# Cross-attention: one score copy moved between two exponentials in ScalarE's program

## The reference, cut to what matters

```python
q = _split_heads(query @ Wq.T + bq, B, Q)      # 16 sequences, 16 heads, 100 queries, 32 dims
k = _split_heads(key @ Wk.T + bk, B, KV)       # 722 keys
v = _split_heads(value @ Wv.T + bv, B, KV)
scores = jnp.einsum('bhqd,bhkd->bhqk', q, k) / SCALE
top_scores, top_idx = jax.lax.top_k(scores, eff_k)      # eff_k = 32
w = jax.nn.softmax(top_scores, axis=-1)
out = jnp.einsum('bhqk,bhqkd->bhqd', w, top_v)
return out @ Wo.T + bo
```

## Time and profile before

| | |
|---|---|
| median of three runs | 2351.82 us |
| the profiled execution, its own time | 2351.33 us |
| its span (first to last instruction) | 2349.5 us |
| PE matmul busy | 2076.7 us, 88% |
| DVE busy | 1954.6 us, 83% |
| ACT busy | 1266.2 us, 54% |
| POOL busy | 1276.8 us, 54% |
| mean granted TensorE clock | 0.951 |
| first and last L1370 (selection) | 815.5 and 2315.3 us |

### The profile page before, as it was taken

How to read it: one execution, slowest core, us unless ns; L and a number is a source line. 1 busy time by engine, 2 the same in 40 slices (tenths; PEclk the granted TensorE clock), 3 DMA queues, 4 the chain that set the end, 5 groups by cost and what they waited for, 6 DMA issues and landing times. The chain is left out here.

```text
span 2349.5 us, 50955 instructions
## 1 busy us (share of the span) xinstructions
PE 2076.7 (88%) x19760; PEld 1630.2 (69%) x19760; DVE 1954.6 (83%) x3663; ACT 1266.2 (54%) x2464; POOL 1276.8 (54%) x1473
## 2 busy tenths in 40 slices
PE   2899999999973789998999999999999999999976
PEld 1566656666641688787887787878777778787754
DVE  4757667675721199999999999999999999999996
ACT  4333333333311266666766666666666666767653
POOL 2565746565512355656656556556655655566533
PEclk9899999999977799999999999999999999999988
DMA  5000000000026110001000010000000100001000
GB/s 187 12 15 23 12 23 12 23 19 19 9 102 153 29 34 13 18 20 31 24 20 25 13 37 18 20 25 24 26 22 16 37 18 20 25 16 35 1 8 11
DMA packets 41500, 70.42 MB, mean 30 GB/s; under 512 B 4638, under 2 KB 21166, under 8 KB 41260
## 3 DMA queue, kind: packets, MB, share of 16 engines
q1 hardware_dynamic: 35868, 56.31, 7.8%
q0 software_dynamic: 3632, 7.58, 1.3%
q10 hardware_dynamic: 1760, 3.28, 0.5%
HBM read 60.54 MB, written 9.86 MB: 30 GB/s over the span
## 5 line engine op out<-in xcount | busy, mean ns | idle before, releaser
L1392 DVE MATCH_REPLACE8 ca_W<-ca_top,ca_W 128x722 f32<-128x722 f32 (+1 forms) x624 | 552.9, 892 | 0.0
L1380 DVE MAX8 ca_top<-ca_W 128x8 f32<-128x722 f32 (+1 forms) x624 | 536.5, 897 | 2.5 <-issue 0.3
L999 POOL TENSOR_TENSOR ca_S<-ca_S,ca_W 128x722 f32<-128x722 f32 (+1 forms) x208 | 358.1, 1742 | 269.7 <-ACT ca_W L1255 269.7
L1255 ACT ACTIVATE ca_W<-ca_W,ca_shift 128x722 f32<-128x722 f32 (+1 forms) x208 | 185.6, 892 | 78.6 <-DVE ca_W L1392 78.5
L976 POOL TENSOR_TENSOR ca_KL<-ca_K,ca_KH 128x384 fp32r<-128x384 f32 (+1 forms) x128 | 122.6, 958 | 188.5 <-ACT ca_KH L1247 186.9
L88 PE MATMUL ca_pS<-ca_KH,ca_QH 128*128 128x362 f32 (+1 forms) x384 | 150.4, 392 | 82.8 <-ACT ca_S L1272 75.0
L1277 ACT ACTIVATE ca_PT<-ca_pT 128x768 f32<-128x768 f32 (+1 forms) x208 | 163.4, 786 | 108.0 <-PE ca_pT L1130 107.9
L1370 DVE MAX8 ca_top<-ca_S 128x8 f32<-128x722 f32 (+1 forms) x208 | 178.9, 896 | 50.1 <-ACT ca_S L1272 49.6
L1163 PE MATMUL ca_pO<-ca_PT,ca_V 128*32 128x56 f32 (+5 forms) x4608 | 217.3, 225 | 0.0
L1265 ACT ACTIVATE ca_S<-ca_S,ca_shift 128x722 f32<-128x722 f32 (+1 forms) x208 | 175.9, 891 | 63.1 <-POOL ca_shift L991 62.9
L362 POOL TENSOR_TENSOR sa_ss<-sa_ss,sa_minus_half 100x16 f32<-100x16 f32 x64 | 187.1, 2941 | 20.0 <-DVE sa_ss L520 20.0
(11 more groups left out here) (213 smaller groups left out, 5183.5 us busy)
## 6 DMA issues: line engine op xcount, KB each, us to landing
ca_raw<-in_ctxT SPq DMA_DIRECT2D x32, 384.0 KB, 4.2
ca_raw<-in_ctxT SPq DMA_DIRECT2D x32, 338.0 KB, 3.0
sa_xin<-in_x SPq DMA_DIRECT2D x16, 200.0 KB
sa_xres<-in_x SPq DMA_DIRECT2D x16, 200.0 KB
x_scratch<-sa_x SPq DMA_DIRECT2D x16, 200.0 KB
x_scratch<-y_scratch POOLq DMA_DIRECT2D x16, 200.0 KB, 13.4
ca_xin<-x_scratch SPq DMA_DIRECT2D x16, 200.0 KB
ca_x<-x_scratch SPq DMA_DIRECT2D x16, 200.0 KB
```

Of the source, the lines that this page charges most:

```text
L999: pool.tensor_tensor(S[k][rows, :], S[k][rows, :], W[r][rows, :], ALU.subtract).then_inc(p_ready, 1)
L1255: act.activation(W[r][rows, :], W[r][rows, :], ACT.Exp, bias=shift[rows, r:r + 1], scale=SCALE).then_inc(f_ready, 1)
L1380: n_of[t.i] = order.mark(dve.max(top[r][rows, 8 * k:8 * k + 8], W[r][rows, :]))
L1392: ins = dve.match_replace(W[r][rows, :], eight, W[r][rows, :], REMOVED)
```

## The change

In steps 0 to 5 ACT now does `exps_left` of the first tile of `last`, then `keep_scores` of `coming[0]`, then `exps_left` of the second tile. Step 6 keeps its order, and where `last` has one tile (step 0) nothing moves.

```diff
                     if old:
                         keep_weights_T(*old[0])
-                    for x in last:
+                    for x in last[:1] if s < 6 else last:
                         exps_left(*x)
...
                     if coming:
                         keep_scores(*coming[0])
+                    for x in last[1:] if s < 6 else []:
+                        exps_left(*x)
                     if s == 5 and nxt:
                         need(act, s_mm, b.count(NT, NT if tiles else 0))
```

## The result

Over 19 runs each on one chip, the kernel before took 2350.36 us in the median and the changed kernel 2357.21 us (2348.34 to 2360.4). The ratio is 1.0025, with a 95% interval of 1.0017 to 1.0034, or +5.9 us (4.0 to 8.0); the two medians are 6.9 us apart. The change makes the kernel slower, by little. In the changed kernel the lines behind the copy are two higher: L1370 is now L1372, L1402 is L1404, L1408 is L1410, L1420 is L1422.

The account below looks back on a forecast made before the run. The prediction took saturated DVE, with stalls behind POOL's subtractions inside its busy time, as the bound. Stall terms 0.1 + 2.2 and L1420's 0.9 gave +3.2 us on 2351.33, plus 0.49 for the median: 2355.0, range 2350.0 to 2358.5.

Parts of the forecast that it names:

- within 0.2%: Whole kernel: time the same as before within 0.2% (4.7 us); chance 0.58.
- DVE bounds, PE's waits don't: Batches 1 to 14: DVE is saturated, busy 93.82 of 94.48 us each, so time PE gets back isn't by itself kernel time.
- The rival by which PE's waits count: 36 waits of PE for the score copy, at most 1.09 us each, save 39 us, giving 2313; chance 0.02.
- The release in step 4: Step 4: the copy releases PE 1.09 us earlier; its first score starts 1.15 instead of 2.24 us after the first L1370.
- The floor: Step 0: p, L984's start after a batch's first selection, can't fall below 12.35 us; there L1402 is held 1.14 us.
- Which batches fall: Of 14: three stay at the floor, five reach it (+3.4 us), half of six late ones too; stall +0.1 and +2.2.
- L1420: Step 4: POOL's second subtraction slips 0.06 us and L1420 with it, 15 times: +0.9 us.
- `QL` and step 5: Step 5: `QL` starts 2.3 us later, tile 0's score 0.4 later; 0.33 of PE's 0.73 wait remains, p untouched.
- From the batches to the whole: Whole kernel: +3.2 us added to the profiled 2351.33 gives 2354.5; the median of the runs is 0.49 higher: 2355.0.
- the likeliest case: Whole kernel: the forecast itself, +3.2 us from longer stalls of L1402 and L1420, 2355.0 us; chance 0.47.
- Caught at the floor: Rival: p is 12.35 to 12.45 in all 14 batches, +4.8 us, with L1420 +5.7: 2357.5; chance 0.30.
- slower: Whole kernel: slower by over 0.2%, over 2356.5 us; chance 0.32.

Follow-up runs that it names:

- e1: The changed kernel run once more, unaltered, for a second profile: ratio 1.0017 to the kernel before.
- e8: Against the kernel before, the copy moved in steps 1, 2, 3 and 5, not in step 4: ratio 0.9994.
- e11: The kernel before run once more, unaltered, for a second profile: ratio 0.9995.
- e2: Against the kernel before, the copy moved in step 4 alone: ratio 1.0043.
- e3: Against the kernel before, the copy moved in step 5 alone: ratio 0.9997.
- e12: The changed kernel with three small ACT copies added ahead of L1232 in step 0, to start L984 later: ratio 1.0042 to the kernel before.
- e4: The changed kernel with L1402's call one place earlier in step 0: ratio 0.9963 to the kernel before.
- e10: Against the kernel before, the copy moved in batch 15 alone: ratio 0.9998.
- e9: Against the kernel before, the copy moved in batches 0 to 14 and not in batch 15: ratio 1.0017.
- e5: The kernel before with only L1402's call one place earlier in step 0: ratio 0.9969.

## Why the prediction was right and wrong

The predicted time was 2355.0 and the measured median 2357.21, inside the range 2350.0 to 2358.5. The direction was right. The size was short: +3.2 forecast, +5.9 (4.0 to 8.0) measured against runs beside it. Part of the closeness of 2355.0 to 2357.21 is luck: the forecast started from 2351.82, the median of three runs, and the 19 runs beside the changed kernel had 2350.36, from which +3.2 gives 2353.6. I had put 0.58 on "within 0.2%", and it came out at 0.25%. Step by step:

*DVE bounds, PE's waits don't.* Right. PE waits 25 us less for the copy, and DVE's busy time alone explains the batches. The rival by which PE's waits count would have given 2313. What PE got back in step 4 it lost waiting for DVE, for keys and for `QL`.

*The release in step 4.* Right: 1.15 against 2.24 us, in every batch, within 0.02.

*The floor.* Right: no p below 12.3 in the changed kernel, and 1.66 to 1.70 at it (1.36 in batch 10). Every held TENSOR_SCALAR of batches 1 to 14 ended 0.28 to 0.29 us behind POOL's instruction, in all profiles that have one, and the selections didn't stretch (no MAX8 or MATCH_REPLACE8 of the changed kernel's first profile took more than 0.92 us). The Trainium skill ("SBUF — State Buffer", section "Who interferes with whom") has the other engine blocked for a whole instruction, and the trace agrees.

*Which batches fall.* Of six late ones half were to reach the floor. That makes eleven with the three and the five; the two profiles show 11 and 10, the others at 13.4 to 15.5. The sum of L1402 and L1408 was to rise by 2.3; it rose by 3.05 and 2.23 in the two. In the first profile the eleven is partly luck: five of the six late ones fell and not three, while batch 7 stayed at 13.5 and batch 11 left the floor for 13.49. In e1 it went nearly as forecast: three late ones fell, the three at the floor stayed, and four of the five joined them.

The step from the release to p was argued in the prediction from two batches. The traces hold more. Take for each batch from 1 to 13 the granted clock over the 10 us behind PE's release in step 4, and the p of the next batch:

| granted clock | p, released at 2.24 (before, e8, e11) | p, released at 1.15 (the change, e1, e2) |
|---|---|---|
| 1.00 | 12.35 to 12.38 | 12.34 to 12.40 |
| 0.83 to 0.86 | 13.24 to 13.55 | 12.35 to 12.38 |
| 0.69 to 0.73 | 14.13 to 14.76 | 13.37 to 13.52 |

So with the earlier release p falls by about 1 us at the same clock, but not below the floor, as forecast. And the full clock is kept more often: behind 3 of the 13 releases in the profile of before, 1 each in e8 and e11, against 9 in the first profile of the change, 6 in e1 and 13 in e2. This line is the window of batch 5 in the changed kernel, to set against 0.70 in the earlier trace rows; the columns are us, busy time of PE, PEld, DVE, ACT and POOL, granted clock, DMA share and GB/s:

```profile
1342.58:1352.58 10.00, 8.70 (x75) 8.16 (x76) 10.00 (x19) 7.34 (x14) 7.63 (x10) 1.00 0.02 5
```

What made the clock stay in one batch and fall in another was not tested.

*L1420.* +0.9 forecast, +1.1 in both.

*`QL` and step 5.* Tile 0's score was to start 0.4 later, with 0.33 left of PE's wait for the copy behind it. From the timeline of the changed kernel ahead of its batch 5, POOL, PE and ACT:

```profile
1268.51 4.55 POOL L1024 TENSOR_TENSOR ca_QL<-ca_qT,ca_QH 32x400 fp32r<-32x400 f32 x4 [0.22 <-issue]
1273.11 0.43 PE L88 MATMUL ca_pS<-ca_KH,ca_QH 128*128 128x362 f32 x1 [0.34 <-POOL ca_QL L1024]
1275.76 0.76 ACT L1272 ACTIVATE ca_S<-ca_pS 128x722 f32<-128x722 f32 x1
1276.57 0.43 PE L88 MATMUL ca_pS<-ca_KH,ca_QH 128*128 128x362 f32 x1 [0.26 <-ACT ca_S L1272]
```

Measured from step 5's first selection, `QL` starts 2.45 later than before (2.3 forecast) and the score 0.58 later (12.37 against 11.79), not 0.4. PE waits 0.34 for `QL`, and 0.26 is left of the 0.73 in the earlier trace rows. The cover holds, by 0.26 us; e3 shows that the time does too.

*From the batches to the whole.* This is the step that fell short. I added the +3.2 of the batches to the profiled execution's time and took everything around them as fixed ("Sum: 0.1 + 2.2 + 0.9 = +3.2 us"). The batches are in order: the two profiles give +4.1 and +3.2. If the other runs' batches are like these two, the missing 2 to 3 us lie before the first selection or behind the last batches; batches are known only for the profiled executions, so this is argued and not shown. These parts move by themselves: over the 14 profiles the first selection comes at 809.3 to 819.7 us with the same code ahead of it (e12 alone has three short copies more), and the time from batch 15 on is 116.7 to 124.4. The changed kernel's 31 runs lie at 2348.3 to 2354.6 and at 2356.1 to 2360.8, and its two profiles are the lowest and the highest of them: of their 12.5 us, 5.1 are before the first selection, 7.8 from batch 15 on, and the batches differ by under 1. Runs of the kernel before can be long too: the 33 beside e1 reach from 2346.03 to 2361.55. Windows of e1 behind its last tile's first selection, which is at 2318.5, show one thing that differs; columns are us, busy time of PE, PEld, DVE, ACT and POOL, and PE's granted clock:

```profile
2328.00:2332.00 4.00, 2.95 (x32) 2.58 (x32) 0.00 (x0) 0.91 (x3) 2.16 (x2) 0.50 0.03 10
2332.00:2336.00 4.00, 3.27 (x41) 2.70 (x39) 0.00 (x0) 0.83 (x2) 1.62 (x2) 0.50 0.02 4
2336.00:2340.00 4.00, 3.25 (x29) 2.02 (x28) 0.22 (x1) 0.27 (x1) 0.00 (x0) 0.50 0.00 0
2340.00:2344.00 4.00, 4.00 (x7) 1.37 (x5) 0.00 (x0) 0.00 (x0) 0.00 (x0) 0.53 0.00 0
```

And windows of the first profile of the changed kernel, where that selection is at 2313.8:

```profile
2320.00:2324.00 4.00, 2.19 (x36) 1.53 (x34) 2.02 (x4) 2.67 (x5) 0.83 (x1) 0.91 0.29 87
2324.00:2328.00 4.00, 2.97 (x69) 2.68 (x70) 0.00 (x0) 0.98 (x3) 3.01 (x4) 1.00 0.00 0
2328.00:2332.00 4.00, 3.26 (x27) 1.62 (x24) 0.22 (x1) 0.27 (x1) 0.00 (x0) 1.00 0.01 4
```

PE's late work runs at 0.50 (1.2 GHz) in the one and at 1.00 (2.4 GHz) in the other. The longest stretch on the lower level is 23.9 us in e1 and 6.8 in the first profile, and the tails differ by 7.8 us. The other profiles fit: the stretch from batch 15's first selection to the last one is 83.8 to 84.0 us in all 14, and behind it the time on the lower level and the length are 10.2 and 32.7 us in the first profile, 13.7 and 34.2 in before, e3, e11 and e12, 20.5 and 36.9 in e4 and e10, 23.9 and 38.1 in e2, 32.3 and 40.5 in e1 and e9. Between these are e5 to e8, with 13.7 to 17.1 and 35.1 to 36.1, so the clock isn't all of it. DVE has hardly anything left to do there, so I read PE's clock as the main cause of the difference; no run set the clock by itself. Whether the change makes the long tail more frequent is open: tails of 122 us and more were seen in e1, e2 and e9, all with the new order in step 4 of the early batches, but not in the first profile or in e12, which have it too. e9 and e10 exclude only that batch 15's own order does it.

So the likeliest case was named rightly as a mechanism and came out 2 to 3 us short in size. "Caught at the floor" gave the nearer number, 2357.5, for a reason that holds in e2 but not quite in the change. A term for the parts outside the batches, with some 3 us either way, would have put more of the chance on "slower".

## What to carry to other kernels

When one engine is saturated and never waits, look for its instructions whose duration varies with the same shape: the stall is inside "busy", and no list of waits shows it. Moving work on another engine then counts only by where it puts the instructions that lock these out, and releasing a waiting engine earlier can line up two engines that missed each other before; moving the held instructions (L1402 one place earlier, L1420 one place later) saved 12 us, while the one try at moving what holds them, e12, went the wrong way. Check after each such move which instruction is next to meet the lock, as e5 shows, and give the parts of the kernel outside the loop a spread of their own.

## What the runs showed of the hardware

- A DVE TENSOR_SCALAR of 100x512 in fp32 took 0.54 us alone and up to 2.08 beside a pair of POOL TENSOR_TENSOR. Where it was held, it ended 0.28 to 0.29 us behind one of POOL's instructions. Of two POOL instructions in a row it waited for the one in which it arrived. Arriving in the first it got in before the second (L984 at 13.53 in batch 2 of before: 1.07 us long, and the pair took 3.78 instead of 3.58). Arriving in the second it waited for the second's end (with L984 at 12.36, 2.19 us before L1404: 1.68 us; in e12, 1.82 behind the start of the pair, just after the second began: 2.05).
- MAX8 and MATCH_REPLACE8 of 128x722 took 0.89 to 0.90 us on average over a kernel in which the same POOL subtractions run beside them, with no hold seen; in before and in the changed kernel's first profile none took more than 0.92.
- PE's granted clock in the last 35 us differed between executions of the same kernel (0.50 or 1.00 some 10 us behind the last first selection), and the ends of the two executions differed by 7.8 us. Nothing run here says what picks it.
